# Half of the MLP's square weights and its output weights, loaded from ScalarE's queue inside expert tiles 15 and 17, with their splitting moved to tiles 19 to 25

## The chip, the core and the metric

The kernel runs on one core of a Trainium2 chip. Its time is the device time of one execution in microseconds (us). Four compute engines matter here: TensorE (PE in the profile, its weight loads PEld), VectorE (DVE), ScalarE (ACT) and GpSimd (POOL). SyncE (SP) only starts transfers. SP and ACT each have a DMA queue of their own; an engine that starts a transfer runs its instructions in order, so a transfer that has to wait for a semaphore holds back all that stands behind it on that engine.

## The reference

Two transformer-like layers on 2048 tokens of width 128, each with a mixer and a feed-forward part, all followed by a layer norm of the residual sum:

```python
x = _layernorm(x + _L0_attn_ref(x, ...))   # gated causal convolution with a small MLP
x = _layernorm(x + _L0_ffn_ref(x, ...))    # mixture of 8 experts, top 2, SwiGLU, hidden 352
x = _layernorm(x + _L1_attn_ref(x, ...))   # attention with exponential features, 16 heads
x = _layernorm(x + _L1_ffn_ref(x, ...))    # MLP with ternary weights:
#   h = silu(x @ w1) * (x @ w2); h = gelu(h @ h1); h = gelu(h @ h2); x = h @ w3   (each with a scale per output)
```

`h1` and `h2` are the two square weights, 512 x 512; `w3` is the output weight, 512 x 128.

## The kernel before

The 2048 tokens are eight batches of 256. The first part runs batch by batch. Each token is then written to two of eight expert regions in DRAM by an indirect DMA of POOL (L493), and the experts work through 39 *tiles* of 128 rows, numbered 0 to 38. SP loads the rows of each tile from DRAM (L397, function `load_rows`), up to three tiles ahead of the transpose that reads them. The tiles come in three phases: the tables that say where the rows of tiles 0 to 8, 9 to 14 and 15 to 38 begin are ready at different moments. `AHEAD` is 15, the number of tiles in the first two phases.

All engines run one `expert_step(t)` after the other, each in its own code, tied by semaphores. In step t TensorE transposes the rows of tile t (L1891), multiplies tile t-1 by the first expert weights (L1695 to L1697), transposes the hidden rows of tile t-3 (L1917) and multiplies tile t-4 by the second weights (L1931). ACT rounds the transposed rows (L765), applies silu (L771) and copies out the answer of tile t-4 (L777). DVE forms the low part of the rows (L1361), the gated product (L1370) and a copy (L1377). The transpose of tile t+1 waits for the low part of tile t. POOL scatters the answer of a tile to DRAM (L595), and from tile 15 on does one small piece of preparation after each (`prepare`): L549 for the attention weights, L554 and L557 for the MLP's input weights (128 x 1024), L560 for the output weights.

The square weights are prepared in the same steps. They come in two transfers of 1 MB, `ff_h[0]` into the room of `x_in` and `ff_h[1]` into the room of `xT_in`. Each holds four pieces of 128 x 512. A piece is split into a high and a low part: ACT writes the high part at the end of step t (L811), DVE subtracts at the end of step t+1 (L1419, which reads both the weights and the high part from SBUF) and scans the low part in step t+2 (L1410). `SPLIT_AT` lists the eight values of t, one for each piece. In step 31 DVE also scans the low part of the input weights (a second L1410, 128 x 1024).

Before, SP's program reads: rows of tiles 12 to 14; `ff_out` (256 KB, L416); `ff_h[0]` (1 MB, L418); wait for the table of the third phase; rows of tile 15 and on, with `ff_h[1]` (L433) after the rows of tile 23.

Of the kernel before, what the change touches and what calls it, by code (L numbers as in the profile page):

```python
# [37 lines left out]
FF_TILES = FF // P  # L38
# [10 lines left out]
AT_RANK = SEQ + 32  # L49
AT_COUNT = AT_RANK + TILES * EXPERTS  # L50
TABLE_STEPS = 16
SPLIT_AT = (15, 17, 19, 21, 27, 29, 31, 33)
EXPERTS_AT = {1: (0, 1), 2: (2, 3), 3: (4, 5), 4: (6, 7)}
LOW_FIRST = {3: 3, 4: 5, 5: 7}
LOW_LAST = {1: (0, 1), 2: (2,), 3: (4,), 4: (6,)}
# [48 lines left out]
def build(nc, A, out):  # L104
# [5 lines left out]
    with ctx:  # L110
# [249 lines left out]
        def _(sp):  # L360
# [45 lines left out]
            for phase in range(PHASES - 1):  # L406
# [3 lines left out]
                for t in range(PHASE_FIRST[phase], PHASE_FIRST[phase + 1], FLY):  # L410
                    load_rows(t, FLY)
                    if t == AHEAD - 2 * FLY:
                        sp.wait_ge(tb["ends"], 1)
                        pads(0, EXPERTS)
            sp.wait_ge(wt["moe_lo"], EXPERTS)
            sp.dma_start(ff_out[:, :, :], A["ff_out"]).then_inc(ld["ff"], 16)  # L416
            sp.wait_ge(g0["res"], BATCHES)
            sp.dma_start(ff_h[0], A["ff_h"][:, 0:FF_TILES, :]).then_inc(ld["ff_h0"], 16)  # L418

            sp.wait_ge(tb["ready"], PHASES)  # L420
            sp.wait_ge(sent_of[PHASES - 1], 16 * TILES * TOP_K * (BATCHES - PHASE_ENDS[-2]))
            sp.wait_ge(wt["zero_rows"], 16 * (EXPERTS + 1))
# [42 lines left out]
        def _(pool):  # L465
# [84 lines left out]

            def split_ff_in(i):
                if i == 0:
                    pool.wait_ge(ld["ff"], 16 * 4)
                    nc.gpsimd.tensor_copy(fi_hi, ff_in).then_inc(wt["fi_hi"], 1)  # L554
                else:
                    pool.wait_ge(wt["fi_hi"], 1)
                    nc.gpsimd.tensor_tensor(fi_lo, ff_in, fi_hi.bitcast(fp32), ALU.subtract).then_inc(wt["fi_lo"], 1)  # L557

            def scaled_out():
                nc.gpsimd.tensor_tensor(ff_out_w[:, :, :], ff_out[:, :, :],  # L560
                                        ff_out_s[:, :].unsqueeze(1).to_broadcast([P, FF_TILES, D]), ALU.mult).then_inc(wt["ff_out"], 1)

# [123 lines left out]
        def _(act):  # L686
# [87 lines left out]
            def answer(u):  # L774
                if live(u, SLOT_TILES):
                    act.wait_ge(mo["down"], u + 1)
                    nc.scalar.activation(routed_row(u)[:, 0:D], ps[:, down_bank(u), 0:D], ACT.Copy).then_inc(mo["out"], 1)  # L777
# [25 lines left out]
            def expert_step(t):  # L803
                high_row(t)
                gate_row(t - 1)
                turned_row(t - 3)
                answer(t - 4)
                if t in SPLIT_AT:
                    r = SPLIT_AT.index(t)
                    act.wait_ge(ld["ff_h0"] if r < FF_TILES else ld["ff_h1"], 16)  # L810
                    nc.scalar.activation(fh_hi[:, r, :], ff_h[r // FF_TILES][:, r % FF_TILES, :], ACT.Copy).then_inc(wt["ff_hi"], 1)  # L811
# [1541 lines left out]
```

## Time and profile before

| | |
|---|---|
| median of 3 runs | 347.21 us (345.64 to 348.92) |
| the profiled execution | 344.88 us |
| its span on the core | 343.1 us |
| PE busy | 313.5 us, 91% |
| DVE busy | 249.8 us, 73% |
| ACT busy | 189.2 us, 55% |
| POOL busy | 161.4 us, 47% |

The span is what the profile covers, from the first instruction to the last; the execution's own time has 1.8 us around it. All times in the profile count from the span's start. The profiled execution is 2.3 us below the median of the runs shown.

### The profile page before, as it was taken

The numbers are of one execution on the slowest core, as the hardware profiler recorded it, in microseconds if no ns is written. First come the engines' busy times: TensorE is split into PE (matmuls) and PEld (weight loads), VectorE is DVE, ScalarE is ACT, GpSimd is POOL, SyncE is SP. The second block draws the span as 40 slices with busy tenths as digits, with TensorE's granted clock in tenths as the row PEclk, the third lists the DMA queues.
The fourth block names the chain that finished last, engine by engine and source line by source line (L and its number), as shares of the span: only waits on it lengthen the run. The fifth ranks groups of instructions, "written<-read, shape, count | busy, mean of one in ns | idle before, by whom it ended". The sixth has DMA issues, their size and how long they took to land.

```text
span 343.1 us, 8922 instructions
## 1 busy us (share of the span) xinstructions
PE 313.5 (91%) x2917; PEld 283.8 (83%) x2917; DVE 249.8 (73%) x852; ACT 189.2 (55%) x401; POOL 161.4 (47%) x221
## 2 busy tenths in 40 slices
PE   7999999988893699999999999999889999999993
PEld 4988988978782599999888776776678999999993
DVE  2577988878890348968985589878995787667844
ACT  3144886654450246646547655654657766767333
POOL 1014577867777445698588584221130433144200
PEclk9999999999998589999999999999999999999998
DMA  6991011122133432522430400000000000000001
GB/s 207 418 403 67 16 34 33 33 54 48 49 71 93 152 111 71 186 63 65 115 96 32 129 14 2 2 3 4 1 2 0 3 15 18 15 15 0 16 18 34
DMA packets 17051, 23.22 MB, mean 68 GB/s; under 512 B 3440, under 2 KB 14448, under 8 KB 16224
## 3 DMA queue, kind: packets, MB, share of 16 engines
q1 hardware_dynamic: 14016, 17.84, 16.3%
q0 software_dynamic: 2272, 4.69, 4.1%
q8 instruction: 24, 0.39, 0.5%
q10 hardware_dynamic: 720, 0.14, 0.2%
q14 instruction: 19, 0.16, 0.1%
HBM read 16.93 MB, written 6.73 MB: 69 GB/s over the span
## 4 chain that ended last, share of the span: by engine, by line
PE 54%; DVE 14%; another core or an unknown queue 4%; issue 4%; ACT 3%; POOL 2%; DVEq 0%; POOLq 0%; ACTq 0%
PE ps L2104 9%; PE ps L2105 9%; PE ps L1931 6%; PE ps L1695 3%; PE ps L1697 3%; PE ps L1917 3%; PE ps L2168 3%; PE ps L1696 3%; PE ps L2026 3%; PE ps L2035 2%; PE ps L2048 2%; PE ps L2065 1%; DVE sb_work L1504 1%; PE ps L1891 1%
## 5 line engine op out<-in xcount | busy, mean ns | idle before, releaser
L2104 PE MATMUL ps<-sb_w_hi,sb_fh_hi 128*128 128x256 f32 x256 | 61.2, 283 | 1.2 <-DVE sb_w_lo L957 0.6
L2105 PE MATMUL ps<-sb_w_lo,sb_fh_hi 128*128 128x256 f32 x256 | 59.9, 278 | 0.0
L2104 PEld LDWEIGHTS ps<-sb_w_hi,sb_fh_hi 128*128 128x128 f32 x256 | 48.2, 188 | 2.4 <-issue 1.1
L2105 PEld LDWEIGHTS ps<-sb_w_lo,sb_fh_hi 128*128 128x128 f32 x256 | 48.2, 188 | 0.0
L1931 PE MATMUL ps<-sb_w,sb_stage 128*128 x234 | 34.6, 286 | 4.6 <-issue 4.6
L493 POOL DMA_INDIRECT routed<-sb_rows_of,sb_row x32 | 32.0, 999 | 11.8 <-issue 8.7
L1931 PEld LDWEIGHTS ps<-sb_w,sb_stage 128*128 128x128 f32 x234 | 30.9, 201 | 5.0 <-issue 4.8
L643 POOL TENSOR_TENSOR sb_w_lo<-sb_x_in,sb_w_hi 128x256 fp32r<-128x256 f32 x24 | 17.5, 754 | 34.9 <-DVE sb_w_hi L1627 34.9
L477 POOL TENSOR_TENSOR sb_veps_h<-sb_mv_h,sb_eps 128x2 f32<-128x2 f32 x16 | 5.1, 318 | 54.5 <-DVE sb_mv_h L970 48.9
L1695 PE MATMUL ps<-sb_w_hi,sb_rT_hi 128*128 x78 | 29.3, 375 | 0.4 <-ACT sb_stage L771 0.4
L595 POOL DMA_INDIRECT answers<-sb_stage x24 | 24.1, 1004 | 11.0 <-ACT sb_stage L777 7.1
L1697 PE MATMUL ps<-sb_w_hi,sb_rT_lo 128*128 x78 | 25.9, 332 | 0.0
L1696 PE MATMUL ps<-sb_w_lo,sb_rT_hi 128*128 x78 | 25.8, 330 | 0.0
L1917 PE MATMUL ps<-sb_const,sb_stage 128*128 128x128 f32 x117 | 20.1, 281 | 4.3 <-ACT sb_stage L783 3.1
L1695 PE MATMUL ps<-sb_front_hi,sb_xT_hi 128*128 128x512 f32 (+1 forms) x64 | 23.2, 362 | 0.7 <-DVE sb_xT_lo L1004 0.7
L595 POOL DMA_INDIRECT answers<-sb_xT_in x15 | 14.4, 960 | 13.9 <-ACT sb_xT_in L777 9.0
L882 ACT ACTIVATE sb_xT_in<-ps,sb_ff_s 128x256 f32<-128x256 f32 x32 | 14.5, 474 | 11.5 <-PE ps L2105 9.0
L874 ACT ACTIVATE sb_work<-ps,sb_ff_s 128x256 f32<-128x256 f32 x32 | 13.9, 474 | 12.5 <-PE ps L2105 12.5
L1696 PE MATMUL ps<-sb_front_lo,sb_xT_hi 128*128 128x512 f32 (+1 forms) x64 | 20.5, 320 | 0.0
L1697 PE MATMUL ps<-sb_front_hi,sb_xT_lo 128*128 128x512 f32 (+1 forms) x64 | 20.5, 320 | 0.0
L1917 PEld LDWEIGHTS ps<-sb_const,sb_stage 128*128 128x128 f32 x117 | 14.6, 144 | 6.3 <-issue 4.0
L891 ACT ACTIVATE sb_x_in<-ps,sb_ff_s 128x256 f32<-128x256 f32 x32 | 14.2, 477 | 9.3 <-PE ps L2105 9.3
(307 smaller groups left out, 928.6 us busy)
## 6 DMA issues: line engine op xcount, KB each, us to landing
sb_stage<-in_w SPq DMA_DIRECT2D x2, 1408.0 KB, 13.9
sb_stage<-routed SPq DMA_DIRECT2D x24, 65.0 KB
sb_w<-in_w SPq DMA_DIRECT2D x1, 1536.0 KB, 18.6
sb_x_in<-in_x_tok SPq DMA_DIRECT2D x1, 1024.0 KB, 9.6
sb_x_in<-in_ff_h SPq DMA_DIRECT2D x1, 1024.0 KB
sb_xT_in<-in_ff_h SPq DMA_DIRECT2D x1, 1024.0 KB
sb_got_first<-answers SPq DMA_DIRECT2D x4, 256.0 KB, 3.4
sb_w<-answers SPq DMA_DIRECT2D x4, 256.0 KB, 4.1
```

The costliest lines, as they stand in the source:

```text
L493: nc.gpsimd.indirect_dma_start(routed[:, :], bass.IndirectOffsetOnAxis(ap=row[:, b, r:r + 1], axis=0), rows_of[:, b, r, :], None).then_inc ...
L595: nc.gpsimd.indirect_dma_start(answers[:, :], bass.IndirectOffsetOnAxis(ap=routed_row(t)[:, AT_DEST:AT_DEST + 1].bitcast(u32), axis=0), ro ...
L643: nc.gpsimd.tensor_tensor(a_lo[:, m, :], f_a[:, m, :], a_hi[:, m, :].bitcast(fp32), ALU.subtract).then_inc(ff["a_lo"], 1)
L882: nc.scalar.activation(f_last[:, m, :], half_bank(6, m), ACT.Gelu, scale=ff_s[:, 3, m:m + 1]).then_inc(ff["g2"], 1)
L891: nc.scalar.activation(f_g[:, m, :], second_bank(b, m), ACT.Gelu, scale=ff_s[:, 2, m:m + 1]).then_inc(ff["g1"], 1)
L1695: mm(dst, lhs[0], rhs[0], start=start, stop=False)
L1696: mm(dst, lhs[0], rhs[1], start=False, stop=False)
L1697: return mm(dst, lhs[1], rhs[0], start=False, stop=stop)
L1917: last = transpose(ps[:, 1, k * P:(k + 1) * P], hid[:, u % FLY, k * P:(k + 1) * P], ident)
L1931: last = mm(ps[:, down_bank(u), 0:D], hidT[:, u % FLY, k * P:(k + 1) * P], w2[:, e, k, :], start=k == 0, stop=k == HIDDEN_TILES - 1)
L2104: mm(dst, w_hi, x_hi, start=start, stop=False)
L2105: last = mm(dst, w_hi, x_lo, start=False, stop=stop and exact)
```

## The change

SP no longer issues the two transfers. ACT issues `ff_h[0]` at the end of step 15 and `ff_out` at the end of step 17. The splits of the pieces 0 to 3 move from steps 15, 17, 19, 21 to steps 19, 21, 23, 25; those of pieces 4 to 7 stay at 27 to 33. POOL's `split_ff_in` now waits for three of the four transfers counted on `ld["ff"]` and `scaled_out` for all four.

```diff
-SPLIT_AT = (15, 17, 19, 21, 27, 29, 31, 33)
+SPLIT_AT = (19, 21, 23, 25, 27, 29, 31, 33)
...
-            sp.wait_ge(wt["moe_lo"], EXPERTS)
-            sp.dma_start(ff_out[:, :, :], A["ff_out"]).then_inc(ld["ff"], 16)
-            sp.wait_ge(g0["res"], BATCHES)
-            sp.dma_start(ff_h[0], A["ff_h"][:, 0:FF_TILES, :]).then_inc(ld["ff_h0"], 16)
-
...
-                    pool.wait_ge(ld["ff"], 16 * 4)
+                    pool.wait_ge(ld["ff"], 16 * 3)
...
             def scaled_out():
+                pool.wait_ge(ld["ff"], 16 * 4)
...
                 answer(t - 4)
+                if t == AHEAD:
+                    act.wait_ge(g0["res"], BATCHES)
+                    act.dma_start(ff_h[0], A["ff_h"][:, 0:FF_TILES, :]).then_inc(ld["ff_h0"], 16)
+                if t == AHEAD + 2:
+                    act.wait_ge(wt["moe_lo"], EXPERTS)
+                    act.dma_start(ff_out[:, :, :], A["ff_out"]).then_inc(ld["ff"], 16)
                 if t in SPLIT_AT:
```

The code below the edit moves, so a line of the kernel before has another number in the changed one: ACT's code is 4 lines higher up (L765 becomes L761), DVE's 2 lines further down (L1361 becomes L1363).

On ACT, at the end of step 15 (behind the answer of tile 11) to the end of step 17, before:

```order
L777 ACTIVATE sb_xT_in<-ps 128x128
L811 ACTIVATE sb_fh_hi<-sb_x_in 128x512
L765 ACTIVATE sb_rT_hi<-ps 128x128
L771 ACTIVATE sb_stage<-ps,sb_stage 128x352
L777 ACTIVATE sb_xT_in<-ps 128x128
L765 ACTIVATE sb_rT_hi<-ps 128x128
L771 ACTIVATE sb_stage<-ps,sb_stage 128x352
L777 ACTIVATE sb_xT_in<-ps 128x128
L811 ACTIVATE sb_fh_hi<-sb_x_in 128x512
```

and the same place now:

```order
L773 ACTIVATE sb_xT_in<-ps 128x128
L806 DMA sb_x_in<-in_ff_h 128x2048
L761 ACTIVATE sb_rT_hi<-ps 128x128
L767 ACTIVATE sb_stage<-ps,sb_stage 128x352
L773 ACTIVATE sb_xT_in<-ps 128x128
L761 ACTIVATE sb_rT_hi<-ps 128x128
L767 ACTIVATE sb_stage<-ps,sb_stage 128x352
L773 ACTIVATE sb_xT_in<-ps 128x128
L809 DMA sb_stage<-in_ff_out 128x512
```

The two splits are replaced by the two transfers, in the same places.

On DVE, from the scan of step 23 to the copy of step 26, before:

```order
L1410 TENSOR_REDUCE sb_odd<-sb_fh_lo 128x1
L1361 TENSOR_TENSOR sb_rT_lo<-ps,sb_rT_hi 128x128
L1370 SCALAR_TENSOR_TENSOR sb_stage<-ps,sb_stage 128x352
L1377 COPY sb_stage<-ps 128x384
L1361 TENSOR_TENSOR sb_rT_lo<-ps,sb_rT_hi 128x128
L1370 SCALAR_TENSOR_TENSOR sb_stage<-ps,sb_stage 128x352
L1377 COPY sb_stage<-ps 128x384
L1361 TENSOR_TENSOR sb_rT_lo<-ps,sb_rT_hi 128x128
L1370 SCALAR_TENSOR_TENSOR sb_stage<-ps,sb_stage 128x352
L1377 COPY sb_stage<-ps 128x384
```

and the same stretch now:

```order
L1412 TENSOR_REDUCE sb_odd<-sb_fh_lo 128x1
L1363 TENSOR_TENSOR sb_rT_lo<-ps,sb_rT_hi 128x128
L1372 SCALAR_TENSOR_TENSOR sb_stage<-ps,sb_stage 128x352
L1379 COPY sb_stage<-ps 128x384
L1421 TENSOR_TENSOR sb_fh_lo<-sb_x_in,sb_fh_hi 128x512
L1363 TENSOR_TENSOR sb_rT_lo<-ps,sb_rT_hi 128x128
L1372 SCALAR_TENSOR_TENSOR sb_stage<-ps,sb_stage 128x352
L1379 COPY sb_stage<-ps 128x384
L1412 TENSOR_REDUCE sb_odd<-sb_fh_lo 128x1
L1363 TENSOR_TENSOR sb_rT_lo<-ps,sb_rT_hi 128x128
L1372 SCALAR_TENSOR_TENSOR sb_stage<-ps,sb_stage 128x352
L1379 COPY sb_stage<-ps 128x384
```

A subtraction now stands in step 24, between the copy L1379 and the low part of tile 25 (L1363), and a scan in step 25; before, steps 24 to 27 had neither.

On POOL nothing moves. Its row in the same stretch, which is the same in both kernels but for line numbers:

```order
L595 DMA answers<-sb_stage 6016x128 x3
L554 CAST sb_front_hi<-sb_conv_bd 128x1024
L595 DMA answers<-sb_stage 6016x128
L557 TENSOR_TENSOR sb_front_lo<-sb_conv_bd,sb_front_hi 128x1024
L595 DMA answers<-sb_stage 6016x128
L560 TENSOR_TENSOR sb_ff_out_w<-sb_stage,sb_ff_out_s 128x512
```

`sb_conv_bd` holds the MLP's input weights here and `sb_front_hi` their high part; L557 follows the answer of tile 19 and reads both from SBUF.

## Rows read from the trace of the kernel before

**Rows 1.** The page: busy shares, TensorE's granted clock by slices of 8.6 us.

```profile
PE 313.5 (91%) x2917; PEld 283.8 (83%) x2917; DVE 249.8 (73%) x852; ACT 189.2 (55%) x401; POOL 161.4 (47%) x221
...
PEclk9999999999998589999999999999999999999998
```

**Rows 2.** Busy time by stretches: us, PE, PEld, DVE, ACT, POOL, clock, DMA, GB/s.

```profile
100.00:120.00 20.00, 10.70 (x52) 9.53 (x51) 6.74 (x23) 3.69 (x11) 12.05 (x13) 0.71 0.43 123
...
140.00:160.00 20.00, 20.00 (x158) 19.89 (x157) 15.66 (x36) 11.10 (x31) 16.31 (x17) 1.00 0.35 112
```

**Rows 3.** The chain that ended last, in order of time, 101 to 116.

```profile
101.48 6.37 another core or an unknown queue
...
110.08 4.93 another core or an unknown queue
```

**Rows 4.** Timeline of SP's queue, 116 to 139.

```profile
116.18 0.42 SPq L418 DMA_DIRECT2D sb_x_in<-in_ff_h  x1
118.65 19.04 SPq L397 DMA_DIRECT2D sb_stage<-routed  x9
138.42 0.34 SPq L433 DMA_DIRECT2D sb_xT_in<-in_ff_h  x1
```

**Rows 5.** Timeline of PE: the transposes of tiles 12, 13, 15 and 16.

```profile
118.05 0.42 PE L1891 MATMUL ps<-sb_const,sb_xT_in 128*128 128x128 f32 x1
...
121.95 0.37 PE L1891 MATMUL ps<-sb_const,sb_xT_in 128*128 128x128 f32 x1
...
126.19 0.27 PE L1891 MATMUL ps<-sb_const,sb_stage 128*128 128x128 f32 x1
...
128.50 0.27 PE L1891 MATMUL ps<-sb_const,sb_stage 128*128 128x128 f32 x1
```

**Rows 6.** Busy time by stretches, while each 1 MB transfer runs.

```profile
116.18:122.00 5.82, 5.82 (x26) 5.75 (x27) 3.79 (x12) 1.60 (x5) 3.83 (x4) 0.50 0.83 282
138.42:144.00 5.58, 5.58 (x45) 5.55 (x44) 4.97 (x12) 3.29 (x10) 3.54 (x4) 1.00 0.80 257
```

**Rows 7.** Timeline of ACT: the split of step 15.

```profile
128.88 0.62 ACT L811 ACTIVATE sb_fh_hi<-sb_x_in 128x512 fp32r<-128x512 f32 x1
```

**Rows 8.** DVE's subtraction by itself (ns min/median/max); then DVE's timeline in step 24.

```profile
L1419 DVE TENSOR_TENSOR sb_fh_lo<-sb_x_in,sb_fh_hi x4: 682/683/750, 131.4 to 143.9; 128x512 fp32r<-128x512 f32 x4
...
148.01 0.28 DVE L1361 TENSOR_TENSOR sb_rT_lo<-ps,sb_rT_hi 128x128 fp32r<-128x128 f32 x1
```

**Rows 9.** Timeline of POOL, 147 to 152.

```profile
147.62 2.40 POOL L557 TENSOR_TENSOR sb_front_lo<-sb_conv_bd,sb_front_hi 128x1024 fp32r<-128x1024 f32 x1
```

**Rows 10.** A DVE line by itself: ns min/median/max; then that instance and POOL's beside it.

```profile
L1495 DVE TENSOR_TENSOR sb_hT<-sb_hT,sb_const x8: 291/311/834, 192.0 to 240.0; 128x128 f32<-128x128 f32 x8
...
205.12 0.83 DVE L1495 TENSOR_TENSOR sb_hT<-sb_hT,sb_const 128x128 f32<-128x128 f32 x1
...
205.07 0.73 POOL L609 TENSOR_TENSOR sb_res<-sb_work,sb_rows_of 128x256 f32<-128x256 f32 x1
```

**Rows 11.** Timeline of DVE and of POOL, 139 to 140.5.

```profile
139.74 0.75 DVE L1419 TENSOR_TENSOR sb_fh_lo<-sb_x_in,sb_fh_hi 128x512 fp32r<-128x512 f32 x1
...
139.19 0.74 POOL L549 TENSOR_TENSOR sb_qk_lo<-sb_qk_w,sb_qk_hi 128x256 fp32r<-128x256 f32 x1
```

**Rows 12.** Timeline of PE and DVE around the wide scan of step 31.

```profile
161.04 0.28 DVE L1361 TENSOR_TENSOR sb_rT_lo<-ps,sb_rT_hi 128x128 fp32r<-128x128 f32 x1
...
161.76 0.27 PE L1891 MATMUL ps<-sb_const,sb_stage 128*128 128x128 f32 x1
...
164.24 0.28 DVE L1361 TENSOR_TENSOR sb_rT_lo<-ps,sb_rT_hi 128x128 fp32r<-128x128 f32 x1
...
164.66 0.30 PE L1891 MATMUL ps<-sb_const,sb_stage 128*128 128x128 f32 x1 [0.66 <-DVE sb_rT_lo L1361]
```

**Rows 13.** Who PE waited for: us in total, times, longest.

```profile
PE ps L1931 <- issue: 4.6, 1, 4.6
...
PE ps L1702 <- POOL sb_euler L471: 1.3, 1, 1.3
```

## The prediction

> **What bounds the kernel now.** I read the page first. TensorE is busy for 91% of the span, the next engine, DVE, for 73%, and TensorE's clock is full but for three slices of 8.6 us from 103 us on [rows 1]. So whatever does not make TensorE wait costs and gives nothing. The stretches show where it does wait: 10.70 of 20 us busy in 100 to 120, against 20.00 of 20 in 140 to 160 [rows 2]. The chain of waits says what the bad stretch is: three pieces whose releaser the profile cannot name, the first from 101.48 on, the last to 110.08 + 4.93 = 115.01 [rows 3]. SP issues `ff_h[0]` at 116.18, with `ff_out` just ahead of it [rows 4]. Both come after the stall, so they cannot be its cause, and taking them away cannot shorten it. The change acts from there on.
>
> **What is removed from SP.** Two issues of 0.42 us. What stood behind them is the load of tile 15's rows, issued at 118.65 [rows 4], which is behind the transpose of tile 12 at 118.05, 0.42 long [rows 5]: a row load waits for the transpose three tiles earlier, and 118.05 + 0.42 is 118.47. So SP was free and waited for TensorE; this load is issued no earlier in the changed kernel. It may land earlier, as it no longer stands behind 1.25 MB: the DMA engines are 0.83 busy in 116.18 to 122.00 [rows 6]. But TensorE reads tile 15 at 126.19, 4 us after the heavy traffic, and tile 16 at 128.50 [rows 5]. The undisturbed period of a tile is 2.08 us: tile 32 follows at 161.76 [rows 12], 16 tiles and 33.26 us later. The interval of 2.31 from tile 15 to 16 exceeds it by 0.23 us. If late rows were the reason, the gain would be 0.23 us; if not, 0. I take 0, and `ff_h[1]` is the test. It is issued at 138.42 ahead of tile 24's rows on the same queue, and the DMA engines are 0.80 busy until 144.00, while TensorE works for 5.58 of those 5.58 us [rows 6] and for 20.00 of the 20 us from 140 on [rows 2], in which it reads tile 24. One megabyte in front of a tile's rows costs TensorE nothing here.
>
> The Trainium skill ("DMA: Bandwidth & Descriptors", section Issuing engines are not separate DMA queues) goes further: transfers started by different engines interleave on the same 16 DMA engines, and another issuing engine saves only the time of issuing. By that rule the gain of the move is the two issues on SP, which no one waits for; by the queue's order it would be up to the 0.23 us above. The trace before has no transfer of this size on ACT's queue to set beside it.
>
> **What is added on ACT.** One issue in step 15 and one in step 17, where a split stood before. The trace has no such issue on ACT at this place; the nearest is SP's of the same transfer, 0.42 us [rows 4], and a split takes 0.62 us [rows 7], so ACT gets 0.2 us shorter in each. The semaphores they wait for (all residuals of the first part, all expert weights split) were already met for SP at 116 us. Steps 19 and 21 keep a split, of another piece. Steps 23 and 25 get one each, 0.62 us; ACT is busy for 11.10 of 20 us there [rows 2], and a split stands behind the answer, where ACT otherwise idles. Cost 0. If that cover were missing, it would be 1.2 us.
>
> **When `ff_h[0]` is there.** Issued where L811 stands now, at 128.88 [rows 7]. The other megabyte took from 138.42 to about 144.0, 5.6 us, the first one from 116.18 to 122.0, 5.8 us [rows 6]. So it lands at about 134.7. Its first reader is the split of step 19, two split positions (four periods, 8.3 us) after 128.88, at 137.2: 2.5 us to spare. `ff_out` follows in step 17, some 4 us after the first, and lands before 137; POOL reads it in L560, behind L557 that ends at 150.02 [rows 9]. Cost 0 for both. Its traffic now lies beside the row loads of tiles 18 to 20; the `ff_h[1]` test above covers that too.
>
> **What moves on DVE: the costly part.** The subtractions leave steps 16 and 18 and come to steps 24 and 26. By busy time alone this is free. A subtraction is 0.68 us long [rows 8], and DVE is busy for 15.66 of 20 us there [rows 2]. But look at what POOL does in step 24. Its L557, 2.40 us long with both inputs in SBUF, runs from 147.62 to 150.02 [rows 9]. What follows DVE's copy starts at 148.01: before, the low part L1361 of tile 25 [rows 8], after the change the subtraction L1421, which also has both inputs in SBUF. Can the two overlap? The trace has such a pair. DVE's L1495 (two inputs in SBUF) takes 311 ns in the median and 834 once; that time it began at 205.12, 0.05 us after POOL's L609 (two inputs in SBUF), which ran to 205.80 [rows 10]. DVE ended at 205.95, 0.15 us behind POOL, although alone it would have ended at 205.43. So DVE stood still until about 0.15 us before POOL's recorded end and then did its work. A second pair agrees: the subtraction at 139.74 overlaps the last 0.19 us of L549, and ends at 140.49 instead of 140.42 [rows 11]; the same model gives 139.93 - 0.15 + 0.68 = 140.46.
>
> Applied to step 24: the subtraction begins at 148.01, POOL having begun 0.39 us before it, and ends at 150.02 - 0.15 + 0.68 = 150.55 instead of 148.69. Delay 1.86 us. The low part of tile 25 stands right behind it, and TensorE's transpose of tile 26, due ten periods after tile 16's at 149.3, waits for that. How much of a DVE delay reaches TensorE is seen in step 31, where the wide scan pushes L1361 from 161.04 + 2.08 = 163.12 to 164.24, by 1.12 us. TensorE's transposes come at 161.76 and 164.66 [rows 12], 2.90 us apart, so 0.82 us is lost and the slack is 0.30. Hence 1.86 - 0.30 = **1.56 us** lost in step 24. The bounds: 0 if DVE and POOL do not meet, 1.86 with no slack. Nothing suggests a gain here. I take 1.56, from the pair of rows that is most like this one.
>
> The Trainium skill ("SBUF — State Buffer", section SBUF: two separate sides) has the rule: a DVE instruction with two SBUF inputs and a GpSimd instruction share a pair of ports under an exclusive lock, and whichever starts second is blocked for all of the other's instruction. By the rule the sum is the one above; if long POOL instructions let DVE in between, as no row of before excludes for one of 2.40 us, both would share and the subtraction would take about twice its 0.68 us, a loss of 0.68 - 0.30 = 0.4 us.
>
> The second new subtraction, two steps or 4.16 us later, would start near 153.7 with TensorE's delay in it. L557 is over, and L560 behind it is smaller by half. Cost 0; if it met L560 as L1495 met L609, some 0.5 us.
>
> **Does the loss reach the end?** Yes: TensorE is busy without a gap around it [rows 2], and attention and MLP take what the experts deliver. The only later gap in these steps, the 0.82 us of step 31, comes from DVE's own queue, which moves along with TensorE.
>
> **Sum.** 344.88 + 1.56 = 346.4 us against the profiled execution, whose 344.88 is 2.33 us below the median of the runs. Against the median, 347.21 + 1.56 = **348.8 us**.
>
> **Rivals.**
> *No meeting, or sharing.* The subtraction is 0.39 us behind L557; a shift by that much the other way would let DVE go first and leave POOL waiting, and sharing costs 0.4. For it: no row shows a 2.40 us block. Against: both engines are tied to TensorE's step. 347.2 to 347.6 us.
> *The gain that the move could bring.* Earlier rows for tile 15 give 0.23 us at most: 347.0. More only if the stall at 101.5 shrinks with the other order of instructions. It lasts 115.01 - 101.48 = 13.5 us; a third less gives 342.7. Its cause is unknown, but it is over before the first changed instruction.
> *Slower through the clock.* The clock fell to half after TensorE had idled 4.6 us; an idle time of 1.3 us near the start is the longest other one [rows 13]. The new gap is 1.56 us, between the two. Its price is that of the last fall: the slices at 0.8, 0.5 and 0.8 [rows 1] make 0.9 x 8.6 / 0.5 = 15 us at half clock, where a tile takes 121.95 - 118.05 = 3.90 us [rows 5] instead of 2.08: 15 x (1 - 2.08/3.90) = 7 us more, 355.8. It decides at once when a gap of 1.56 us is enough. Against: the gap is much nearer to 1.3 than to 4.6.
> *Late weights.* If `ff_h[0]` on ACT's queue took over 8.3 us instead of 5.8, ACT, and TensorE behind it, would wait for the rest; at 12 us, twice as long, 3.7 us: 352.5.
>
> **How the numbers follow.** The block as computed: 0.61. No meeting or sharing: 0.19. A real gain through the stall: 0.07. Clock, late weights or a longer stall: 0.13. About 1% (3.5 us) is what a measurement of this kernel can tell from no change: 343.7 and 350.7 are the bounds. The first two cases are within them but for scatter: same 0.78, slower 0.14, faster 0.08. The runs of before scatter by -1.6 and +1.7 us around their median. From 347.2 - 1.6 for the second case to 348.8 + 1.7 for the first, with a little of the slower ones: 345.5 to 351.0.
>
> **What the changed profile would show.** L1421 in step 24 near 2.5 us long, beginning 0.4 us behind POOL's L552 (L557 before), the others near 0.68. TensorE waiting some 1.5 us for DVE's L1363 before the transpose of tile 26, and no wait before that of tile 15. The three nameless pieces from 101.5 as before. `ff_h[0]` issued near 128.9, no ACT wait in step 19. It would be wrong if the nameless stall changes its length, or if L1421 stays short.

## The result, and the profile after

The changed kernel takes 346.23 us in the median of 20 runs (342.60 to 348.90), the kernel before 344.66 us in 20 runs on the same chip (342.42 to 348.92, and one of 388.11). The ratio is **1.0054, 95% interval 1.003 to 1.0077**: slower by 1.9 us (1.0 to 2.6). The ratio leaves out the runs over 1.5% above the fastest of their kernel (of the changed one 348.28, 348.78 and 348.90), so it says a little more than the 1.57 us between the two medians. The forecast 348.8 was 1.56 us, a ratio of 1.0045, above a median of three runs that turned out 2.5 us above the median of twenty.

The profiled execution takes 347.65 us, its span is 345.7 us. The page, busy times and granted clock, against [rows 1]:

```profile
PE 312.6 (90%) x2917; PEld 283.1 (82%) x2917; DVE 251.4 (73%) x852; ACT 189.5 (55%) x401; POOL 161.8 (47%) x221
...
PEclk9999999999995698999999999999999999999998
```

DVE is busy 1.6 us longer with the same 852 instructions. One of them has grown. DVE's timeline in step 24, against [rows 8]:

```profile
148.10 0.55 DVE L1379 COPY sb_stage<-ps 128x384 f32<-128x384 f32 x1
148.56 2.55 DVE L1421 TENSOR_TENSOR sb_fh_lo<-sb_x_in,sb_fh_hi 128x512 fp32r<-128x512 f32 x1
151.03 0.28 DVE L1363 TENSOR_TENSOR sb_rT_lo<-ps,sb_rT_hi 128x128 fp32r<-128x128 f32 x1
```

POOL's timeline there, against [rows 9]:

```profile
148.17 2.39 POOL L552 TENSOR_TENSOR sb_front_lo<-sb_conv_bd,sb_front_hi 128x1024 fp32r<-128x1024 f32 x1
```

PE's timeline there, the transposes of tiles 25 and 26, against [rows 5, 12]:

```profile
147.80 0.27 PE L1893 MATMUL ps<-sb_const,sb_stage 128*128 128x128 f32 x1
151.46 0.30 PE L1893 MATMUL ps<-sb_const,sb_stage 128*128 128x128 f32 x1 [1.41 <-DVE sb_rT_lo L1363]
```

The subtraction of 0.68 us lasts 2.55. It ends at 151.11, 0.55 us behind the recorded end of POOL's instruction (148.17 + 2.39 = 150.56), as -0.15 + 0.68 gives +0.53. Tile 26 follows tile 25 after 3.66 us and tile 27 after 2.15, where before both took 2.07: 1.67 us are lost.

A second place differs. PE's transposes of tiles 16 to 18, then the ACT rows ahead of them:

```profile
125.28 0.27 PE L1893 MATMUL ps<-sb_const,sb_stage 128*128 128x128 f32 x1
130.50 0.42 PE L1893 MATMUL ps<-sb_const,sb_stage 128*128 128x128 f32 x1
133.28 0.27 PE L1893 MATMUL ps<-sb_const,sb_stage 128*128 128x128 f32 x1
```

```profile
124.10 0.27 ACT L761 ACTIVATE sb_rT_hi<-ps 128x128 fp32r<-128x128 f32 x1
126.80 0.55 ACT L767 ACTIVATE sb_stage<-ps,sb_xT_in 128x352 f32<-128x352 f32 x1 [2.43 <-PE ps L1699]
126.94 0.34 ACTq L806 DMA_DIRECT2D sb_x_in<-in_ff_h  x1
```

ACT stands still for 2.43 us in front of the silu of step 15, and the transfer is issued behind that halt, not ahead of it. That the issue stands behind the halt in time rules it out as the halt's cause. The granted clock then falls to half for 3.40 us (windows, columns as in [rows 2]):

```profile
128.60:132.00 3.40, 3.40 (x15) 3.40 (x16) 1.38 (x4) 0.49 (x2) 0.86 (x2) 0.50 0.78 304
```

Where the difference of the two profiles lies can be read from TensorE's transposes. From tile 0 to tile 38 it is 97.91 us before (77.19 to 175.10) and 102.68 after (74.64 to 177.32), 4.77 more: 3.05 from tile 10 to tile 18 (30.81 and 33.86), 1.67 at tiles 26 and 27. But tile 0 began 2.55 us earlier, and in all 19 profiles that start falls between 73.9 and 75.0 or between 77.2 and 77.7, whatever the kernel. So a single pair of profiles says little on a difference of 1.9 us; its places have to be tried one by one.

### The profile page after: what moved, and what is told of

It is laid out like the page before. It is cut to its first block, busy times and chain, and to the rows that moved or that the text cites. A ratio compares the mean times of both kernels' runs of the same rounds, so it can differ in the third digit from the quotient of the medians.

```text
span 345.7 us, 8922 instructions
## 1 busy us (share of the span) xinstructions
PE 312.6 (90%) x2917; PEld 283.1 (82%) x2917; DVE 251.4 (73%) x852; ACT 189.5 (55%) x401; POOL 161.8 (47%) x221
## 4 chain that ended last, share of the span: by engine, by line
PE 54%; DVE 15%; issue 7%; ACT 3%; POOL 2%; DVEq 0%; POOLq 0%; ACTq 0%
PE ps L2106 10%; PE ps L2107 9%; PE ps L1933 6%; PE ps L1699 3%; PE ps L1697 3%; PE ps L2170 3%; PE ps L1698 3%; PE ps L1919 3%; PE ps L2028 2%; PE ps L2037 2%; PE ps L2050 2%; PE ps L2067 1%; DVE sb_work L1506 1%; PE ps L1893 1%; PE ps L2003 1%
## 5 line engine op out<-in xcount | busy, mean ns | idle before, releaser
L1697 PE MATMUL ps<-sb_front_hi,sb_xT_hi 128*128 128x512 f32 (+1 forms) x64 | 22.4, 349 | 1.1 <-DVE sb_xT_lo L1006 1.1
L1363 DVE TENSOR_TENSOR sb_rT_lo<-ps,sb_rT_hi 128x128 fp32r<-128x128 f32 x39 | 11.0, 283 | 12.4 <-issue 9.5
L1698 PE MATMUL ps<-sb_front_lo,sb_xT_hi 128*128 128x512 f32 (+1 forms) x64 | 19.8, 309 | 0.0
L1699 PE MATMUL ps<-sb_front_hi,sb_xT_lo 128*128 128x512 f32 (+1 forms) x64 | 19.8, 309 | 0.0
```

Source lines behind the costliest of these rows:

```text
L1697: mm(dst, lhs[0], rhs[0], start=start, stop=False)
L1698: mm(dst, lhs[0], rhs[1], start=False, stop=False)
L1699: return mm(dst, lhs[1], rhs[0], start=False, stop=stop)
```

## The experiments

Two kinds of chips were met. On some, all kernels have the nameless stall of [rows 3] at tiles 10 to 12 and take some 345 us (the runs above, e5 to e8, e16 and e17). On the others there is none and they take some 332 us (e1 to e4, e9 to e15). I call them chips with and without the stall. Ratios are always to the kernel before on the same chip.

### The two kernels again, and the parts of the change (e1 to e4, without the stall)

e1 is the kernel before, e2 the changed kernel, both as they are.

> The kernel before once more, for a second profile. Theory 1 (the cost of the change is the subtraction of step 24, held up by POOL's 2.40 us piece): here no subtraction stands in step 24, all eight take 0.68 to 0.83 us, and the transposes of tiles 25 to 27 are 2.07 apart. Theory 2 (the cost is a stall of ACT around steps 14 to 17, which the changed kernel's profile shows at 124.4 to 126.8 and which the issues on ACT bring): the transposes of tiles 14 to 18 take no more than the 8.6 us of the first profile of this kernel. If instead they take 11 to 12 us here too, that stall is not the change's.

> The changed kernel once more, profile and 5 rounds. Theory 1: the subtraction of step 24 again takes about 2.5 us and the transposes of tiles 25 and 26 are about 3.65 apart; 1.003 to 1.008 of before. Theory 2: the transposes of tiles 14 to 18 again take 12.3 us instead of 8.6; if they take under 9.5 us, the stall is one of the first profile alone.

e3 is the changed kernel with POOL's preparation from `split_ff_in(1)` on one tile later:

```diff
                 if t >= AHEAD - 1:
-                    prepare(t - AHEAD + 1)
+                if t >= AHEAD - 1 and t != 19:
+                    prepare(t - AHEAD + 1 - (t > 19))
```

> The changed kernel with POOL's preparation from the low part of the input weights on moved one tile later (nothing is prepared behind tile 19's answer), so that the 2.40 us piece runs from about 149.3 to 151.7 on the old clock, between the subtractions of steps 24 and 26. Theory 1: the subtraction of step 24 takes 0.68 us again, the transposes of tiles 25 and 26 are 2.07 to 2.1 apart, and the kernel gets back about 1.6 us: 0.998 to 1.002 of before. Theory 2 (issues on ACT are what costs): no gain, still 1.003 to 1.008.

e4 is the kernel before with the new list of splits alone; SP issues both transfers as before:

```diff
-SPLIT_AT = (15, 17, 19, 21, 27, 29, 31, 33)
+SPLIT_AT = (19, 21, 23, 25, 27, 29, 31, 33)
```

> The kernel before with the list of split steps alone changed (19, 21, 23, 25, 27 and on); both transfers stay on SP ahead of tile 15's rows. Theory 1: all of the cost is here, the subtraction of step 24 takes about 2.5 us, 1.003 to 1.008 of before. Theory 2: no ACT issue, so no cost but what DVE shows: 0.998 to 1.002 and an undisturbed step 24 would be needed for it to be the whole explanation.

| | time, us | ratio, 95% |
|---|---|---|
| e1, before | 333.61, one run; 332.03 median of 29 | |
| e2, changed | 333.35 | 1.0038 (1.0008 to 1.0068) |
| e3, changed, POOL one tile later | 331.07 | 0.9992 (0.9956 to 1.0028) |
| e4, split list alone | 334.37 | 1.0061 (1.0024 to 1.0098) |

**The held subtraction.** e4 has it with ACT issuing nothing: DVE, then POOL.

```profile
138.21 2.55 DVE L1419 TENSOR_TENSOR sb_fh_lo<-sb_x_in,sb_fh_hi 128x512 fp32r<-128x512 f32 x1
```

```profile
137.82 2.37 POOL L557 TENSOR_TENSOR sb_front_lo<-sb_conv_bd,sb_front_hi 128x1024 fp32r<-128x1024 f32 x1
```

e3 has the change without it. Its subtraction by itself (ns min/median/max):

```profile
L1421 DVE TENSOR_TENSOR sb_fh_lo<-sb_x_in,sb_fh_hi x4: 681/682/700, 123.9 to 137.9; 128x512 fp32r<-128x512 f32 x4
```

Tile 26 follows after 2.09 us, and e3 is faster than e2 by 2.3 us in the medians (by the means of the runs behind the two ratios 1.9 us, 95% interval 0.9 to 2.9). So the term is shown from both sides, with the change and without its transfers on ACT. Theory 2 fails in e2: the transposes of tiles 14 to 18, which took 12.31 us in the profile after, take 8.28 us.

In the profile of e2 the term is larger, as DVE's recorded start is 0.10 us ahead of POOL's and it is held all the same. DVE, POOL, and TensorE's transpose of tile 26:

```profile
136.60 3.02 DVE L1421 TENSOR_TENSOR sb_fh_lo<-sb_x_in,sb_fh_hi 128x512 fp32r<-128x512 f32 x1
```

```profile
136.70 2.37 POOL L552 TENSOR_TENSOR sb_front_lo<-sb_conv_bd,sb_front_hi 128x1024 fp32r<-128x1024 f32 x1
```

```profile
139.97 0.30 PE L1893 MATMUL ps<-sb_const,sb_stage 128*128 128x128 f32 x1 [1.86 <-DVE sb_rT_lo L1363]
```

The clock was at half behind it, for 3.4 us, and tile 27 came 3.75 us later instead of 2.07, 1.68 us more. This execution took 337.04 us, 3.7 us above e2's median, so its larger loss is not the usual one. The stretch behind tile 26 (windows):

```profile
140.20:143.70 3.50, 3.50 (x16) 3.43 (x16) 2.39 (x7) 0.83 (x2) 2.69 (x4) 0.51 0.19 57
```

**What I had not forecast.** e1, the kernel before. SP's timeline, POOL's, then PE's:

```profile
106.22 0.42 SPq L416 DMA_DIRECT2D sb_stage<-in_ff_out  x1
106.69 0.42 SPq L418 DMA_DIRECT2D sb_x_in<-in_ff_h  x1
113.32 1.38 SPq L397 DMA_DIRECT2D sb_stage<-routed  x3
```

```profile
107.11 0.96 POOL L493 DMA_INDIRECT routed<-sb_rows_of,sb_row  x1 [0.30 <-issue]
```

```profile
111.44 0.27 PE L1891 MATMUL ps<-sb_const,sb_xT_in 128*128 128x128 f32 x1
115.20 0.33 PE L1891 MATMUL ps<-sb_const,sb_stage 128*128 128x128 f32 x1 [1.52 <-DMA sb_stage<-routed]
```

Without the stall TensorE waits for the rows of tile 15: 3.76 us instead of 2.07, 1.7 lost. In e2 tile 15 follows after 2.08. There the move does gain what it takes off SP, but not because the rows stood behind a megabyte in the queue. Once issued they land fast: TensorE starts 1.9 us after the issue (113.32 to 115.20). It is the issue that is late. In front of it SP waits, at L422 (L417 in the changed kernel), for POOL's scatters (L493) that put the rows of the third phase in DRAM; the description of SP's program above leaves this wait out. SP's waits, e1 then e2:

```profile
SPq L422 <- DMA routed<-sb_rows_of,sb_row: 5.3, 1, 5.3
```

```profile
SPq L417 <- DMA routed<-sb_rows_of,sb_row: 3.1, 1, 3.1
```

POOL starts the last of these scatters at 107.11 in both, and the rows of tile 15 are issued at 113.32 in e1 and at 110.31 in e2. The DMA engines from 108 to 111, e1 then e2 (windows):

```profile
108.00:111.00 3.00, 3.00 (x25) 2.82 (x24) 1.37 (x4) 1.36 (x4) 2.08 (x4) 1.00 1.01 399
```

```profile
108.00:111.00 3.00, 3.00 (x25) 2.96 (x24) 1.47 (x4) 1.32 (x4) 2.09 (x4) 1.00 0.13 44
```

So `ff_out` and `ff_h[0]`, under way at that moment, hold up POOL's scatters, which are on another queue, and these hold up SP. Every run without the stall agrees: from the start of the last scatter to the issue of tile 15's rows it is 6.1 to 7.4 us where the two transfers go out just before (e1, e4, e9, e10, e13, e14) and 3.2 to 3.4 us where they go out later, from either engine (e2, e3, e11, e12, e15).

But e2 gives it back nine tiles later. SP, then PE at tiles 23 and 24:

```profile
128.36 0.34 SPq L428 DMA_DIRECT2D sb_xT_in<-in_ff_h  x1
129.58 5.05 SPq L397 DMA_DIRECT2D sb_stage<-routed  x4
```

```profile
130.12 0.27 PE L1893 MATMUL ps<-sb_const,sb_stage 128*128 128x128 f32 x1
133.70 0.33 PE L1893 MATMUL ps<-sb_const,sb_stage 128*128 128x128 f32 x1 [1.34 <-DMA sb_stage<-routed]
```

`ff_h[1]` waits on SP for POOL's stores of tiles 0 to 14, whose backlog ends at the same time in e1 (issue at 128.37) and e2 (128.36), while TensorE is 1.7 us further on in e2. Tile 24's rows stand behind it: SP issues them at 129.58, 3.6 us after the transpose of tile 21 (125.97) that they would otherwise wait for, and they take 4.1 us more with the megabyte just ahead of them. They come 1.5 us late. e1 issues them at 129.59 and has no wait there, since its TensorE is later. e3 has the gain and the new wait without the collision, and its ratio is 0.9992.

### Taking away the second wait, and two tests of the first term (e5 to e8, with the stall)

Their expectations were written for a chip without the stall, and the four ran on one with it. e5 is e3 with `ff_h[1]` behind the rows of tiles 24 to 26:

```diff
-                if t == AHEAD + 2 * FLY:
+                if t == AHEAD + 3 * FLY:
```

> The changed kernel with POOL's preparation one tile later, as in the run before, and with ff_h[1] issued on SP behind the rows of tiles 24 to 26 instead of ahead of them. Theory: in the two runs of the changed kernel on this chip TensorE waits 1.3 to 1.5 us for the rows of tile 24, because they stand on SP's queue behind ff_h[1], whose issue waits for POOL's stores and comes no earlier than before. Behind tile 26 the megabyte is in nobody's way: the transpose of tile 24 follows that of tile 23 after about 2.1 us instead of 3.5, and the time is 1.3 us below the kernel with POOL's shift alone, ratio to before 0.995 (0.992 to 0.998). With that TensorE has neither the wait of tile 15 nor that of tile 24 nor the held subtraction. Rival: the wait is only handed on, to the rows of tile 27, which now stand behind the megabyte: then the interval to tile 27 is over 3 us and the ratio stays near 0.999.

e6 is e5 with both transfers on SP, behind the rows of tiles 15 to 17; ACT's two issues are gone:

```diff
                 load_rows(t, FLY)
+                if t == AHEAD:
+                    sp.wait_ge(g0["res"], BATCHES)
+                    sp.dma_start(ff_h[0], A["ff_h"][:, 0:FF_TILES, :]).then_inc(ld["ff_h0"], 16)
+                    sp.wait_ge(wt["moe_lo"], EXPERTS)
+                    sp.dma_start(ff_out[:, :, :], A["ff_out"]).then_inc(ld["ff"], 16)
```

> The kernel of the run above, but ff_h[0] and ff_out stay on SP's queue, behind the rows of tiles 15 to 17 instead of ahead of them; ScalarE issues nothing. Theory: what matters is which rows stand behind a transfer on one queue, not which engine issues it. Tile 15 has no wait as with ScalarE's queue, and the rows of tile 18 have three tiles, 6.2 us, to land behind 1.25 MB that take about 6 to 7 us: a wait of 0 to 1 us at tile 18. Ratio equal to the run above within 0.003, so 0.993 to 0.998. Rival: a queue of its own is worth something by itself (transfers of two queues share the engines, those of one stand in line): then rows of tile 18 come 2 us or more late and the ratio is 1.001 or more.

e7 is the changed kernel with e5's edit alone. e8 is the changed kernel with POOL's subtraction in two:

```diff
-nc.gpsimd.tensor_tensor(fi_lo, ff_in, fi_hi.bitcast(fp32), ALU.subtract).then_inc(wt["fi_lo"], 1)
+for w in range(2):
+    nc.gpsimd.tensor_tensor(fi_lo[:, w, :], ff_in[:, w, :], fi_hi[:, w, :].bitcast(fp32), ALU.subtract).then_inc(wt["fi_lo"], 1)
```

> The changed kernel with only ff_h[1] moved behind the rows of tiles 24 to 26; POOL's order is the changed kernel's, so the subtraction of step 24 still meets POOL's 2.4 us subtraction. Theory: the terms add. The wait of tile 24 (1.3 to 1.5 us) goes, the held subtraction (2.5 to 3.0 us long, 1.5 us lost) stays, and the ratio to before is 1.0038 - 0.0042 = 0.9996 (0.997 to 1.003). Rival: removing the wait of tile 24 shifts DVE and TensorE against POOL, whose stores do not wait for those rows, so that the two subtractions no longer meet in the same way: the subtraction is about 0.7 us long and the ratio 0.995; or they meet earlier and it stays at 3.0 us.

> The changed kernel with POOL's one subtraction of 128x1024 written as two of 128x512, about 1.2 us each; nothing else differs. Theory: POOL holds DVE off for one instruction at a time. DVE's subtraction of step 24, which begins 0.1 us ahead to 0.4 us behind POOL's, gets in between the halves: it ends at the first half's end - 0.15 + 0.68, so it is 1.3 to 1.8 us long instead of 2.5 to 3.0, TensorE loses 0.4 to 0.9 us instead of 1.5 to 2.1, and the ratio to before is 1.0005 (0.998 to 1.003) against 1.0038 of the changed kernel. Rival one: POOL's second half follows before DVE gets the port, the subtraction stays at 2.5 to 3.0 us and the ratio at 1.004. Rival two: the long subtraction was not held by POOL's at all but by transfers into the same memory; then halves change nothing either, and its end is not tied to POOL's.

| | time, us | ratio, 95% | longest subtraction |
|---|---|---|---|
| before | 345.07 | | |
| e5, no collision, `ff_h[1]` later | 345.35 | 1.0000 (0.9966 to 1.0033) | 0.85 |
| e6, the same, all on SP | 344.94 | 0.9979 (0.9943 to 1.0016) | 0.76 |
| e7, collision, `ff_h[1]` later | 346.24 | 1.0021 (0.9984 to 1.0058) | 2.54 |
| e8, collision, two halves | 347.23 | 1.0036 (0.9998 to 1.0075) | 2.70 |

Here the kernel before does not wait at tile 15, so there is nothing to gain, and e5 and e6 come out even with it. The collision is worth the same on this kind of chip: the mean ratio of the three kernels with it (1.0054, 1.0021, 1.0036) is 1.0037, of the two without 0.999, 1.6 us apart. On the chip of e5 to e8 alone, the runs behind the ratios of e7 and e8 average 1.6 us more than those of e5 and e6 (95% interval 0.9 to 2.2); the single intervals are too wide to tell e7 from e5.

e8 was a miss. POOL (two instructions in a row, 2.54 us together), then DVE:

```profile
148.87 2.54 POOL L553 TENSOR_TENSOR sb_front_lo<-sb_conv_bd,sb_front_hi 128x512 fp32r<-128x512 f32 x2
```

```profile
149.26 2.70 DVE L1422 TENSOR_TENSOR sb_fh_lo<-sb_x_in,sb_fh_hi 128x512 fp32r<-128x512 f32 x1
```

DVE did not get in between the halves. It ends at 151.96, again 0.55 us behind the end of POOL's second half at 151.41: rival one, with POOL going from one instruction to the next before DVE's turn. Its ratio of 1.0036 fits rival one as well.

### Again without the stall (e9 to e12)

e9 and e10 are the kernel before, e11 is e5 and e12 is e6, unchanged.

> The kernel before, unchanged, for its profile. On the chip of the last four runs all four changed kernels and the changed kernel itself stood still on ScalarE for 2.4 to 2.6 us in front of the silu L767 of step 16, whether or not ScalarE issues a transfer there; the one profile of the kernel before on that chip has a halt of 1.6 us one place earlier and a regular interval of 2.2 us between the transposes of tiles 16 and 17, where the changed ones have 4.5 to 5.4. Theory one: the halt belongs to the chip and to the load of instructions just ahead of it, and its length is not set by the change; then this profile has one of 1.1 to 2.6 us there too, and the five changed ones were not dearer for it. Theory two: without a split in steps 15 and 17 ScalarE's halt is longer by 1 us or more and costs TensorE 2 to 3 us; then the transposes of tiles 15 to 18 are again near 2.2 us apart here, with one of about 2.3. If the run falls on the other chip, there is no halt at 100 to 115 us, and TensorE waits 1.5 us for the rows of tile 15.

> The same kernel once more, for the scatter of the same places: the start of tile 0 (74.6 or 77.3 us), the interval from tile 10 to tile 18 and the halt on ScalarE in steps 15 and 16. Theory one: the interval from the transpose of tile 10 to that of tile 18 differs from the run before it by over 1 us where a halt is in it. Theory two: both give 30.8 us within 0.5 on the chip with the halts, against 32.8 to 34.2 of the changed kernels.

> The changed kernel with POOL's preparation one tile later and ff_h[1] behind the rows of tiles 24 to 26, again. On the chip without the halt, where the kernel before loses 1.7 us at tile 15, neither that wait, nor the one of tile 24, nor the held subtraction is left: ratio 0.995 (0.991 to 0.998). Rival, and what to expect on the chip with the halt, where the kernel before has none of the three: 1.000 (0.996 to 1.003), as in the run there.

> The kernel in which ff_h[0] and ff_out stay on SP's queue behind the rows of tiles 15 to 17, again, beside the one above on the same chip. If only the place in the row of loads matters and not the queue, the two ratios agree within 0.003, 0.995 on the chip without the halt and 0.999 on the other. Rival: one queue for all costs tile 18 a wait for its rows of over 1 us, and this kernel is slower by 0.003 or more.

| | time, us | ratio, 95% | wait for rows of tile 15 / 18 / 24, us |
|---|---|---|---|
| e9, before | 330.47, one run | | 1.7 / 0 / 0 |
| e10, before | 332.17, one run; 331.62 median of 23 | | 2.65 / 0 / 0 |
| e11 = e5 | 330.08 | 0.9962 (0.9928 to 0.9996) | 0 / 0 / 0 |
| e12 = e6 | 330.23 | 0.9955 (0.9923 to 0.9988) | 0 / 1.68 / 0 |

Both beat the kernel before by 1.3 to 1.5 us. The wait of tile 24 is gone, as expected. In e12 the rows of tile 18 stand behind the two transfers. PE's transposes of tiles 17 and 18:

```profile
114.84 0.27 PE L1892 MATMUL ps<-sb_const,sb_stage 128*128 128x128 f32 x1
118.75 0.33 PE L1892 MATMUL ps<-sb_const,sb_stage 128*128 128x128 f32 x1 [1.68 <-DMA sb_stage<-routed]
```

That is longer than the 0 to 1 us that I had expected, and near the rival's 2 us: rows issued at 111.24, 1.8 and 1.3 us behind the two transfers (109.45 and 109.93), are late. e11 does not show the opposite for ACT's queue, though: its rows of tile 18 are issued at 113.37, ahead of ACT's megabyte (115.21). The two runs differ in the moment of the transfer and not only in its queue, and the times do not tell them apart. So whether a queue of its own is worth something stays open. e11's profile also lost time elsewhere: it waited 1.96 us for the rows of tile 12, the clock was at half for 3.4 us behind that, and tiles 13 and 14 came after 3.07 and 2.75 us. And its subtraction of step 20 met another piece of POOL (L544, 0.74 us), lasted 1.24 us, and cost 0.37 us at tiles 22 and 23. In e6, on the chip with the stall, tile 18 did not wait, but tile 27, whose rows stand behind `ff_h[1]` there, waited 0.6 us; in e5 and e11 it did not.

### A longer halt on ACT: the change's or the chip's? (e13 to e17)

All five profiles of changed kernels on chips with the stall (after, e5 to e8) have a halt of ACT of 2.4 to 2.6 us in front of the silu of step 15, e6 too, where ACT issues nothing. (The expectations place it in step 16: counted from the order of the instructions it is step 15.) e13 and e16 are the kernel before, e14 and e17 are e4, e15 is the changed kernel.

> The kernel before, for its profile, to be set beside the five profiles of changed kernels that have a halt of ScalarE of 2.4 to 2.6 us in front of the silu of step 16. Theory one (the halt belongs to the chip and an instruction load just ahead of it): on a chip with halts this profile has one of over 2 us in steps 15 to 17 as well, with the interval from tile 10 to tile 18 over 32.5 us. Theory two (the halt is longer because steps 15 and 17 have no split): 1.6 us or less of halt and 30.8 us from tile 10 to tile 18. On a chip without halts the interval is 20.2 us and this run tells nothing on it.

> The kernel before with the changed list of splits alone. On a chip with halts, theory two expects the long halt in front of the silu of step 16 here as well, theory one expects no tie to the list. On a chip without halts: as the run of this kernel before, a subtraction of 2.5 us in step 24.

> The changed kernel again. On a chip with halts: the halt of 2.4 us in front of the silu of step 16, the held subtraction of 2.55 us, no wait for the rows of tile 24, ratio 1.005. On a chip without: no halt, no wait at tile 15, one of 1.3 us at tile 24, the held subtraction, ratio 1.004.

> The kernel before, for its profile, once more in search of a chip with halts. There, theory one (the halt of ScalarE in step 15 or 16 belongs to the chip) expects over 2 us of halt and over 32.5 us from the transpose of tile 10 to that of tile 18; theory two (it is longer where steps 15 and 17 have no split) expects 1.6 us or less and 30.8 us. On a chip without halts: 20.2 to 21.5 us, with 1.5 to 2.7 us of waiting for the rows of tile 15.

> The kernel before with the changed list of splits alone. On a chip with halts theory two expects a halt of 2.4 us in front of the silu of step 16, theory one no tie to the list. On any chip: a subtraction of 2.5 us in step 24 and 3.6 us from the transpose of tile 25 to that of tile 26, unless DVE's subtraction begins over 0.1 us ahead of POOL's.

e13 to e15 fell on a chip without the stall and say nothing on the halt: 334.36, 331.96, and 331.63 us with a ratio of 1.0000 (0.9969 to 1.0030). But they bear on the rest. e13 and e14 wait 1.8 us for the rows of tile 15, e15 does not, and waits 1.47 us at tile 24. e14 has the held subtraction, 2.55 us, and so has e17 below; tile 26 follows after 3.65 us in both. e15 misses its forecast: not 1.004 but 1.0000, and its profile shows that the meeting of step 24 can fail to come about. DVE's subtractions of steps 24 and 26, then POOL:

```profile
133.49 0.68 DVE L1421 TENSOR_TENSOR sb_fh_lo<-sb_x_in,sb_fh_hi 128x512 fp32r<-128x512 f32 x1
...
137.65 1.88 DVE L1421 TENSOR_TENSOR sb_fh_lo<-sb_x_in,sb_fh_hi 128x512 fp32r<-128x512 f32 x1
```

```profile
134.30 2.40 POOL L552 TENSOR_TENSOR sb_front_lo<-sb_conv_bd,sb_front_hi 128x1024 fp32r<-128x1024 f32 x1
...
137.87 1.10 POOL L556 TENSOR_TENSOR sb_ff_out_w<-sb_stage,sb_ff_out_s 128x512 f32<-128x512 f32 x1
```

DVE was 0.81 us ahead in step 24 and done before POOL began. Two steps later its subtraction met POOL's L556 and ended at 139.53, 0.56 us behind it (138.97); tile 28 followed after 2.99 us instead of 2.07 and tile 29 after 2.16. This profile lost 1.0 us in this way, where the profile after lost 1.67 at tiles 26 and 27.

e16 (342.66 us) and e17 (345.43 us) have the stall. The halts there are in front of other instructions. ACT in e16, then in e17:

```profile
121.33 0.55 ACT L771 ACTIVATE sb_stage<-ps,sb_xT_in 128x352 f32<-128x352 f32 x1 [2.11 <-PE ps L1697]
122.83 0.28 ACT L777 ACTIVATE sb_xT_in<-ps 128x128 f32<-128x128 f32 x1 [0.94 <-remote]
```

```profile
125.61 0.28 ACT L777 ACTIVATE sb_xT_in<-ps 128x128 f32<-128x128 f32 x1 [2.37 <-remote]
```

From the transpose of tile 10 to that of tile 18 it is 30.81 (before), 31.22 (e16) and 31.20 us (e17); with the changed order of loads 33.86 (after), 34.17, 34.11 and 34.19 (e5, e7, e8), and 32.75 (e6). So a halt of over 2 us comes in the kernel before as well (e16), against theory two; the split list alone does not make the stretch longer (e17), which disposes of theory two. But the profiled changed kernels lose 1.5 to 3.4 us more there, against theory one. The timed runs do not bear such a loss out: e5 has that stretch of 34.17 us in its profile and no other loss but 0.45 us at tile 31, yet its median is 0.3 us above that of before, with an interval of 1.1 us to either side. That part stays open, and with it whether the new order of loads costs anything on such a chip beyond the held subtraction.

## Why the prediction was right in one term and wrong in another

**What bounds the kernel.** Right: each loss and gain above is a wait of TensorE, or a clock at half behind one. ACT's issue of `ff_h[0]` took 0.34 us and held no one up in the profile after. ACT's halt of 2.4 us in front of it did cost TensorE time there; what makes it is open.

**Moved on DVE, 1.56 us.** Right. The profile after shows 2.55 us where "near 2.5" was said, an end at +0.55 where +0.53 was worked out, and 1.67 us lost. e4 has the term alone, e3 the change without it. The same +0.55 to +0.56 fits e2, e4, e7, e8, e14, e15, e17 and the profile after. The rule of the Trainium skill ("SBUF — State Buffer", section SBUF: two separate sides) that went with it, that the one that starts second is blocked for the whole of the other's instruction, holds in these runs, and sharing is excluded. By recorded starts it would have let DVE go first in e2, where DVE is 0.10 us ahead and is held; the measurement decides, and the recorded start is not the moment that counts there. In e12 it goes the other way round: DVE's subtraction of step 20 (125.79 to 126.76) is 0.33 us ahead of POOL's L549, whose 0.74 us become 1.24, with an end 0.60 us behind DVE's.

**"The second new subtraction: cost 0."** Right in most runs (0.77 us in the profile after). e15 shows the bound that was given with it, "if it met L560, some 0.5 us", as 1.0 us, twice the bound.

**The step that failed: "About 1% (3.5 us) is what a measurement of this kernel can tell from no change", and "same 0.78" built on it.** The sum named a loss of 1.56 us and gave it 0.61, and this step turned that loss into "same". Twenty runs of each kernel tell 0.24%, 0.8 us, to either side. They show a loss of 0.54%, 1.9 us (1.0 to 2.6), and the mechanism is the one in the sum: 1.67 us at tiles 26 and 27 of the profile after, absent where POOL's piece is moved (e3, e5, e6). The argument for 1.56 us should have led to "slower, by about half a per cent".

The level was off too. The median of three runs stood 2.5 us above that of twenty, which is why 348.8 is 2.6 us above 346.23. That the difference of 1.56 us lies within 0.3 us of the measured one is partly luck: the profiles of the changed kernel on such chips also lose up to 3.4 us around tile 17 that the timed runs do not show and that no run explains.

**"What is removed from SP ... I take 0", and its test, "one megabyte in front of a tile's rows costs TensorE nothing here".** On the chip of the result this came out right: tile 15 follows after 2.07 us before and 2.23 after, tile 24 after 2.07 and 2.06. As a statement on the kernel it is wrong, and what hid it was the stall. There TensorE reads tile 15 at 126.19, 7.5 us after the issue of its rows at 118.65, and SP waits for no scatter. Without the stall the two transfers just before cost the kernel before 1.5 to 2.65 us of waiting (e1, e9, e10, e13, e14; 0.6 in e4, which had lost time just ahead), by way of POOL's scatters, and the change takes that away (e2, e3, e15). Then the tested megabyte itself costs 1.3 to 1.5 us at tile 24 (e2, e3, e15), because its issue waits for POOL and TensorE has become earlier. With e5's edit that is gone (e11). The prediction took a wait of zero for a property of the queue; it was slack, and the change spends slack. It also asked only what stands behind the transfers on SP's own queue, and not what else is under way beside them.

The rule weighed beside that step, of the Trainium skill ("DMA: Bandwidth & Descriptors", section Issuing engines are not separate DMA queues), says that transfers started by different engines run on the same 16 DMA engines and interleave, and that another issuing engine saves only the time of issuing. The runs agree with the first half: SP's two transfers delay POOL's scatters by 2.7 to 4.2 us (e1 against e2 and the others above). The second half did not settle the gain, because the change moved the transfer in time as well, from 106.69 in e1 to 115.83 in e2; no run issues the same transfer at the same moment from either engine.

**Rivals.** "No meeting" came in step 24 in one of three profiles of the changed kernel (e15); three are too few to judge the 0.19, and sharing is excluded. The clock: a gap of 1.4 us did not lower it, as forecast (the profile after, clock 1.00 from 147.8 to 156.0). Where it fell behind longer waits it was for 3.4 us and cost 1.7 us (e2), not the 15 us and 7 us of the rival's price, which came from the fall at the stall. That one lasted 13.65 us in the kernel before (108.48 to 122.13), a little less than the 15 read off the slices. Late weights: no run had them. The stall did not change with the order of instructions; it went with the chip.

## What to carry to other kernels

A row of no wait in a profile is slack at that moment, not a price of zero: if a change makes the reader earlier, or takes away a stall ahead of it, ask again what stands in front of its load, and put a large transfer behind the loads that are needed before it. Look beyond its own queue: here it delayed small scatters of another engine, and a third waited for these. Before calling a small loss "same", ask what the number of runs can tell; here it was 0.24%. Before work with two SBUF inputs is moved to a place on DVE, look at what POOL runs there, back-to-back instructions taken as one; moving POOL's piece by one tile gave back the whole loss (e3). The best version found, splits moved, POOL's piece one tile later and `ff_h[1]` behind tile 26 (e5, e11), is 0.4% faster than the kernel before on chips without the stall and level with it on chips with it. The form with both transfers left on SP, behind the rows of tile 17, does as well (e6, e12), so the gain comes from the place and does not need ACT.

## What the runs showed of the hardware

- The same program takes some 345 us on some chips and 332 on others. The difference is a stall of ACT and SP of 13 us at tiles 10 to 12 and what follows it: of the 11.3 us between the profiles of the kernel before and e1, 10.6 lie between the transposes of tiles 10 and 18. The instruction loads of that place are in both: two of 8 KB between 97 and 102 us in the kernel before with the stall and in e1 without it (the instruction queue by itself, packets, MB, share):

```profile
q14 instruction: 2, 0.02, 0.8%
```

```profile
q14 instruction: 2, 0.02, 1.1%
```

  What makes the stall was not found.
- DVE held by POOL ends 0.55 to 0.56 us behind POOL's recorded end in each case, for an own time of 0.68 us. In the one case tried, POOL's next instruction, following without a gap, went first (e8).
- Two transfers, 1.25 MB together, on SP's queue delayed the landing of POOL's scatters, on another queue, by 2.7 to 4.2 us (e1, e4, e9, e10, e13, e14 against e2, e3, e11, e12, e15).
- After a gap of TensorE the clock was at half for 3.4 us behind waits of 1.9 to 2.4 us (e2, e4, e11), and not at all behind one of 2.65 us (e10). The length of the gap alone does not decide it.
